# A DMA queue reordered within its slots, and three ScalarE copies a slot later

## Time and profile before

| | us |
|---|---|
| median of three runs | 5356.7 |
| lowest and highest | 5356.41, 5357.89 |
| the profiled execution | 5352.76 |
| its span, first to last instruction | 5351.0 |
| PE busy | 4918.7 (92%) |
| DVE busy | 4686.7 (88%) |
| POOL busy | 3950.9 (74%) |
| ACT busy | 2777.2 (52%) |

### The profile page before, as it was taken

How to read it: one execution, slowest core, us unless ns; L and a number is a source line. 1 busy time by engine, 2 the same in 40 slices (tenths; PEclk the granted TensorE clock), 3 DMA queues, 4 the chain that set the end, 5 groups by cost and what they waited for, 6 DMA issues and landing times.

```text
span 5351.0 us, 80535 instructions
## 1 busy us (share of the span) xinstructions
PE 4918.7 (92%) x22532; PEld 3287.7 (61%) x22532; DVE 4686.7 (88%) x5835; ACT 2777.2 (52%) x4594; POOL 3950.9 (74%) x2047
## 2 busy tenths in 40 slices
PE   5899999999999799899999999989999999999967
PEld 2688888888888455555555555555555555555544
DVE  9676766767676699999999999999999999999997
ACT  3111111111111576777677677777667776767754
POOL 5233333333332599999999999999999999999996
PEclk9999999999999899999999999999999999999979
DMA  4111111111110423323233333333333333323222
GB/s 117 48 44 41 45 39 45 41 43 43 39 47 32 128 88 111 102 92 108 87 122 101 91 104 110 98 102 94 115 95 99 107 92 111 110 81 114 80 91 66
DMA packets 286369, 444.72 MB, mean 83 GB/s; under 512 B 39521, under 2 KB 100961, under 8 KB 281746
## 3 DMA queue, kind: packets, MB, share of 16 engines
q1 hardware_dynamic: 285970, 440.23, 26.2%
HBM read 350.94 MB, written 89.17 MB: 82 GB/s over the span
## 4 chain that ended last, share of the span: by engine, by line
DVE 18%; PE 17%; issue 14%; ACT 8%; POOL 7%; DVEq 1%; DMA 1%; SPq 0%; POOLq 0%; ACTq 0%
DVE hs L1434 11%; DVE acc L1448 6%; POOL v L1193 5%; PE mm L1567 4%; PE ht L1579 4%; ACT decay L1392 3%; PE mm L1508 3%; PE mm L1499 3%; PE mm L1516 2%; POOL hw L1203 1%; PE yw L1589 1%; PE mm L1551 1%; DVEq L1019 1%; DMA b_rep<-ssm_d 1%; ACT L1279 1%
## 5 line engine op out<-in xcount | busy, mean ns | idle before, releaser
L1193 POOL TENSOR_TENSOR v<-u,b_rep 128x1024 f32<-128x1024 f32 x1024 | 2401.2, 2365 | 150.2 <-DVE hs L1434 68.1
L1392 ACT ACTIVATE decay<-dt,a_neg 128x512 f32<-128x512 f32 x2048 | 1389.7, 688 | 657.0 <-DVE hs L1434 644.7
L1579 PEld LDWEIGHTS ht<-ident,hs 128*128 128x128 f32 x6400 | 784.8, 144 | 1013.9 <-issue 662.6
L1434 DVE TENSOR_TENSOR_SCAN hs<-decay,carry,v 128x512 f32<-128x512 f32 x1024 | 1285.2, 1273 | 34.9 <-POOL hw L1203 19.5
L1434 DVE TENSOR_TENSOR_SCAN hs<-decay,v 128x512 f32<-128x512 f32 x1024 | 1230.6, 1221 | 49.2 <-ACT decay L1392 38.3
L1448 DVE SCALAR_TENSOR_TENSOR acc<-ht,c_now,acc 128x512 f32<-128x512 f32 x1600 | 1173.3, 733 | 17.4 <-PE ht L1579 16.5
L1579 PE MATMUL ht<-ident,hs 128*128 128x128 f32 x6400 | 1005.0, 281 | 179.3 <-DVE hs L1434 83.6
L683 ACT ACTIVATE sg<-gate 128x512 f32<-128x512 f32 (+1 forms) x192 | 108.1, 563 | 1339.9 <-PE up L723 1339.9
L1203 POOL TENSOR_TENSOR hw<-hs,c_rep 128x512 f32<-128x512 f32 x448 | 572.1, 1277 | 10.4 <-DVE hs L1434 10.4
L1567 PE MATMUL mm<-w_out,yt 128*128 128x512 f32 x1024 | 513.0, 605 | 8.7 <-ACT xb L1264 5.2
L1516 PE MATMUL mm<-w_in,x_z 128*128 128x512 f32 x1024 | 508.6, 601 | 6.7 <-ACT acc L1318 6.7
(11 more groups left out here) (157 smaller groups left out, 7971.0 us busy)
## 6 DMA issues: line engine op xcount, KB each, us to landing
b_rep<-ssm_d SPq DMA_DIRECT2D x512, 256.0 KB, 3.5
w_out<-in_L_attn_W_out SPq DMA_DIRECT2D x32, 1024.0 KB, 7.8
rtb<-res_d SPq DMA_DIRECT2D x128, 256.0 KB, 4.1
tap_diag<-tap_d SPq DMA_DIRECT2D x120, 256.0 KB, 3.5
c_rep<-ssm_d SPq DMA_DIRECT2D x448, 64.0 KB, 3.4
xt<-in_L_attn_x SPq DMA_DIRECT2D x64, 256.0 KB, 2.7
xn_d<-xn SPq DMA_DIRECT2D x64, 256.0 KB, 2.0
rt<-in_L_attn_x SPq DMA_DIRECT2D x64, 256.0 KB, 2.6
```

Source lines behind the costliest of these rows:

```text
L1193: nc.gpsimd.tensor_tensor(v[k % 2][:, j:j + 2, :], u[g][:, j:j + 2, :], b_rep[k % 3][:, :].unsqueeze(1).broadcast_to([P, 2, CL]), ALU.mult ...
L1392: nc.scalar.activation(decay[n % 3][:, :], dt[g][:, j, :], ACT.Exp, scale=a_neg[:, GD * g + j, s:s + 1]).then_inc(decay_ready, 1)
L1434: nc.vector.tensor_tensor_scan(h[k % 3][:, j, :], decay[n % 3][:, :], v[k % 2][:, j, :], carry[:, s, GD * g + j:GD * g + j + 1] if c.secon ...
L1579: last = nc.tensor.transpose(ht[add_no[k, t] % 2][:, j, :], h[k % 3][:, j, t * P:(t + 1) * P], ident[:, :])
```

## The change

In `SP_AT` "x_store" moves from slot 1 to slot 3, and in slot 27 the load of the residual stands ahead of row block 1. In SP's `part` the moves "row" (except row block 3), "x_store" and "x_z" are taken out of the slot's first part and issued at its end, behind `load_c` and `load_b`. So slot 31 is: row block 3, C's row, B's row for slot 1 of the next chunk, x_z. In `ACT_AT` three copies out of PSUM move by one step: projection 6 from n = 60 to 61, gate block (0, 2) from 81 to 82, gate block (1, 0) from 116 to 117.

```diff
-              54: [("xd", 1, 3)], 57: [("cv", 4)], 60: [("ip", 6)], 63: [("cv", 5)], 66: [("ip", 7)],
+              54: [("xd", 1, 3)], 57: [("cv", 4)], 61: [("ip", 6)], 63: [("cv", 5)], 66: [("ip", 7)],
...
-              76: [("silu_xc", 6), ("silu_xc", 7)], 78: [("z", 0, 1)], 81: [("z", 0, 2)],
+              76: [("silu_xc", 6), ("silu_xc", 7)], 78: [("z", 0, 1)], 82: [("z", 0, 2)],
...
-              113: [("xd", 0, 2), ("relu", 0, 2)], 114: [("relu", 0, 3), ("tr", 1)], 116: [("z", 1, 0)], 120: [("z", 1, 1)],
+              113: [("xd", 0, 2), ("relu", 0, 2)], 114: [("relu", 0, 3), ("tr", 1)], 117: [("z", 1, 0)], 120: [("z", 1, 1)],
...
-    SP_AT = {1: [("x_store",)], 2: [("w_out", 1), ("load", 1, 0), ("load", 1, 1)], 5: [("tap", 2)], 7: [("tap", 3)], 8: [("store", 1, 0)],
+    SP_AT = {2: [("w_out", 1), ("load", 1, 0), ("load", 1, 1)], 3: [("x_store",)], 5: [("tap", 2)], 7: [("tap", 3)], 8: [("store", 1, 0)],
...
-             26: [("store", 0, 1), ("load", 0, 2)], 27: [("row", 1), ("load", 0, 3)], 28: [("store", 0, 2)], 29: [("row", 2), ("store", 0, 3)],
+             26: [("store", 0, 1), ("load", 0, 2)], 27: [("load", 0, 3), ("row", 1)], 28: [("store", 0, 2)], 29: [("row", 2), ("store", 0, 3)],
...
         def part(c):
             for k in range(SLOTS):
+                turns = [what for what in SP_AT.get(k, ()) if what[0] in ("row", "x_store", "x_z") and what != ("row", 3)]
                 for what in SP_AT.get(k, ()):
-                    move(c, *what)
+                    if what not in turns:
+                        move(c, *what)
                 if c.exists(NC) and k in weigh_no:
                     load_c(c, k)
                 if k + 2 < SLOTS:
...
                 elif c.plus(1).exists(NC):
                     load_b(c.plus(1), k + 2 - SLOTS)
+                for what in turns:
+                    move(c, *what)
```

## The result

| | before | after |
|---|---|---|
| median, us (6 runs each) | 5356.56 | 5332.59 |
| lowest and highest | 5354.74, 5357.89 | 5330.43, 5332.99 |
| the profiled execution | 5352.76 | 5332.94 |
| its span | 5351.0 | 5331.2 |

The ratio is 0.9956, with a 95% interval from 0.9945 to 0.9966. The mechanism is looked at first, and the missing 12 us after it.

The account below looks back on a forecast made before the run. The prediction took DVE (busy 219.1 us of 225) and POOL (218.5 us) to bound the second phase. Its terms, 4.6 + 4.4 + 3.1 = 12.1 us, off the median 5356.7 gave 5345 us, range 5339.5 to 5355.

Parts of the forecast that it names:

- B's row for slot 1, before x_z: At chunk starts, issuing this row earlier removes POOL's 2.05 us stand; DVE gains 4.6 us at s4 and s5.
- zero at the back edges: At the starts of chunks 4, 6, 8, 10 and 12, DVE's own way round the loop sets s0: gain 0.
- The wait behind it: At n = 13, DVE's wait for turned states, delayed by PE's wait for POOL's gated half of y, goes: 4.4 us.
- B's row for slot 29: Issued before the second row of x, it ends POOL's pause there; s0 of the next chunk gains, 3.1 us together.
- The store of the turned copy: Moved from slot 1 behind slot 3's loads; nobody else waits for it until slot 26: cost 0.
- The rows of x behind: Behind B's row, rows 1 and 2 go when they went, row 0 one or two DMA issues later: cost 0.
- the three ACT copies: One slot later, a decay is made during ACT's wait for PE, but no scan waits for those decays: gain 0.
- The sum: Whole kernel: 12.1 us off the profiled 5352.76 gives 5340.7; carried to the median 5356.7, 5344.6, or 5345 us.
- Rival 1: At chunk starts the wait passes from POOL to ACT and PE; only 5.4 us won, 5351 us; chance 0.24.
- Rival 2: At the three later ACT copies PE waits for a bank; slower, 31 us less 12, 5376 us; chance 0.07.
- Rival 3: B's row is late for its broadcast to 128 partitions, not its place; no change, 5356.7 us; chance 0.12.
- Rival 4: In odd chunks the clock falls in other places, -2.8 to +2.8 us; better side 5341 us taken, chance 0.12.

Follow-up runs that it names:

- h1: The kernel after, with x_z loaded in slot 2 of its own chunk instead of slot 31 of the one before: 5327.05 us, ratio 0.9948.
- k_xz_quarter: The kernel before, order unchanged, but x_z loads only 256 KB of its 1 MB: 5333.39 us, ratio 0.9957.
- l1_pool_late: The kernel after, with POOL making the first half of v twice in slot 1 of every chunk: 5356.66 us, ratio 1.0002.
- e2: The kernel before, with only row blocks 0 to 2 of x behind B's row and slot 27's residual load ahead of row block 1: 5355.66 us, ratio 0.9997.
- e5: The kernel after, with the store of the turned copy back in slot 1: 5333.48 us, ratio 0.9955.
- e3: The kernel before, with only the store of the turned copy moved from slot 1 to the end of slot 3: 5348.93 us, ratio 0.9985.
- e4: The kernel before, with only the three ACT copies moved one step later: 5356.47 us, ratio 0.9999.

## Why the prediction was wrong

By its own steps:

- *B's row for slot 1, before x_z*, 4.6 us at s4 and s5: right in place and size (16.7 to 12.1 us in the profiled executions; from the second profile of before it is 18.8 to 12.1, so that it is right to the tenth is luck), with s5 floored 8.60 us behind s0, as it said. Its zero at the back edges was nearly right in the sum (1.2 us) and wrong in its reason: h1 and k_xz_quarter show that the transfer of x_z makes most of that lateness.
- *The wait behind it*, 4.4 us at n = 13: the step that failed, as the term that was mis-sized: it measured 6.9 + 2.7 = 9.6 us. The wait went as it said, but it was priced by its listed idle time. From s8 to s24 chunk 5 took 27.82 us before and 27.30 after, 0.52 us for a listed wait of 0.34; over chunks 1 to 15 the stretch from n = 13 gave 6.9 us rather than 4.4. And the step ended there. It asked what DVE wins at the next wait of PE for POOL, and not how long POOL stays late: until n = 62, worth 2.7 us more. l1_pool_late brings both back, 7.8 and 2.2 us.
- *B's row for slot 29*: 3.7 us at s0 against 3.1, right. That it is worth nothing alone (e2) and something beside the row for slot 1 was not said; the prediction added its terms as if each stood alone.
- *The store of the turned copy*, 0: right beside the row (e5), wrong alone (e3, 7.9 us).
- *The rows of x behind*, *the three ACT copies*: 0 and 0, right (e2, e4).
- *The sum* failed too, by 4.2 us. The profiled execution of before was 3.8 us under its median, and the difference was carried over unchanged. It isn't a constant: the second profiled execution of that kernel lay 1.5 us under its median (it lost 2.1 us more at s4 and s5), and the profiled execution of after lay 0.3 us over its own. So 4.2 of the 24.0 us between the medians are not in the 19.8 us between the two spans. 12.1 + 4.2 = 16.3, and what the terms missed (2.5, 2.7, 1.9, 1.2, 1.0 and 0.6, less 2.2) makes the rest, 24.0. Why the two distances differ is open.
- *The rivals.* Rivals 1, 2 and 3 are out: POOL's stand went and nothing took its place, PE waits for no bank, and the time is not the old one. Rival 4, the clock, acted in one place where it had not been looked for, the end. In every trace PE stands 2.3 us for the last scan, and again, 1.0 to 2.2 us, for the gated y. In the kernel before the turned states behind the first of these pauses take 1.36 us at a granted 1.00, and the lower clock comes behind the second: in the stretch from 5327 to 5332 us it is 0.73, and the eight output products take 5.05 us. In the kernel after it comes behind the first, where the turned states take 1.97 us at 0.50, and is over when the output products come: 1.00 and 3.67 us. That is 1.4 of the 1.9 us at the end. 0.73 is a mixture of the two levels, 1.2 and 2.4 GHz; 0.50 is the lower one.

Before, then after:

```profile
5320.61 1.36 PE L1579 MATMUL ht<-ident,hs 128*128 128x128 f32 x8 [2.30 <-DVE hs L1434]
...
5326.95 5.05 PE L1567 MATMUL mm<-w_out,yt 128*128 128x512 f32 x8 [0.31 <-ACT yt L1324]
...
5327.00:5332.00 5.00, 5.00 (x9) 2.26 (x10) 0.00 (x0) 0.34 (x1) 0.65 (x1) 0.73 0.00 0
```

```profile
5301.51 1.97 PE L1583 MATMUL ht<-ident,hs 128*128 128x128 f32 x8 [2.31 <-DVE hs L1438]
...
5308.46 3.67 PE L1571 MATMUL mm<-w_out,yt 128*128 128x512 f32 x8 [0.40 <-ACT yt L1328]
...
5308.00:5312.00 4.00, 3.60 (x10) 1.66 (x10) 0.00 (x0) 0.81 (x2) 1.16 (x1) 1.00 0.00 0
```

The Trainium skill, page "TensorE: Matmul & The Clock Gate", Part 1, says that the gate's windows run freely; by that the same pause can fall on either side of one. The traces agree: the same 2.3 us has the lower clock right behind it in ten of the sixteen and not in the other six. It does not go with POOL's lateness alone: k_xz_quarter, whose POOL is on time at slot 1 or within 0.2 us of it, has 4.91 us for the products, and e4, whose POOL is late, has 4.71 us with the fall behind the first pause. So these 1.4 us can't be put down to what the edit does to POOL.

What stays open: why 1 MB behind B's row in the queue delays the row (e3), and how the transfer of x_z makes DVE's first scan behind the back edge late (the packets of instructions are there; that they are what is late was not tried). Nor was x_z issued from another engine's queue, which would tell the order in one queue from the sharing of the DMA engines.

## What to carry to other kernels

Put the small load that a full engine needs next in front of the bulk load in its queue, and price its stand by all that this engine's lateness touches until it has caught up, not by the first wait behind it: here 2 us of POOL at slot 1 showed at s4, at n = 13 and at n = 50 to 62. To measure such a price directly, make the engine late by a known amount in the finished kernel (one product made twice gave it in one run). Losses far apart add up and losses that meet at one place don't; of a profiled execution look first at how far it lies from its median, since that distance isn't a constant to be carried over.

## What was not expected of the hardware

- A load of 1 MB under way at the loop's back edge makes DVE's first scan behind it late: 2.7 to 3.1 us with it, 0.9 in chunk 6 with it moved away, in all five 14.8 against 4.9 us. At the same edges the DMA engines carry packets of instructions, 8 in the 12.8 us ahead of chunk 6.
- A row of 256 KB behind 1 MB in the queue landed 6.4 us after its issue; with a store of 1 MB behind it taken away, 5.2 us; with a quarter of the bytes ahead of it, 3.8 us; the median of its kind is 3.5 us.
- The same pause of PE, 2.3 us for the last scan, was followed at once by the lower clock in ten traces and not in six; the eight output products behind it took 3.67 us in nine of the ten, and 4.9 to 5.1 us in the six.
